# Moving the load of the next queries behind the round trip of denominators on SyncE's queue

## The reference, cut to what matters

```python
x = x + layernorm(attn(layernorm(x)))
x = x + layernorm(ffn(layernorm(x)))
# attn, for each of 16 heads of 32 numbers:
q_phi = exp(features(q) - |q|^2 / 2)            # 128 features
S, sum_k = k_phi^T v, sum over rows of k_phi    # per sequence
out = (q_phi S) / max(q_phi sum_k, eps)         # a denominator for each row and head
attn = concat(out) w_out^T
# ffn: sigmoid gates, top 4 of 32 experts, capacity 512, plus a shared expert
```

## Time and profile before

| | |
|---|---|
| median of 3 runs | 2131.26 us (2128.41 to 2144.04) |
| the profiled execution, its time | 2139.98 us |
| the profiled execution, its span | 2138.2 us |
| mean granted TensorE clock in it | 0.939 of full speed |
| fused stage, about | 862 to 1417 us of the span |

### The profile page before, as it was taken

How to read it: one execution, slowest core, us unless ns; L and a number is a source line. 1 busy time by engine, 2 the same in 40 slices (tenths; PEclk the granted TensorE clock), 3 DMA queues, 4 the chain that set the end, 5 groups by cost and what they waited for, 6 DMA issues and landing times.

```text
span 2138.2 us, 33516 instructions
## 1 busy us (share of the span) xinstructions
PE 1843.4 (86%) x12976; PEld 892.7 (42%) x12976; DVE 1183.8 (55%) x2055; ACT 1071.0 (50%) x1371; POOL 756.9 (35%) x716
## 2 busy tenths in 40 slices
PE   8899999999988999699789888635998999987785
PEld 6444444444436888133233333322444444443231
DVE  7676766666650000156778878762444444445786
ACT  5555554545524666566566666412444444432443
POOL 0000000000000000013578787875677777761110
PEclk9999999999998999899899999867999999998897
DMA  6636354454527888567887785443799999987983
GB/s 231 232 124 239 132 193 178 168 203 165 178 103 209 211 212 205 120 175 188 225 221 239 220 235 183 161 183 100 169 197 221 247 241 246 205 146 241 334 288 126
DMA packets 197295, 421.92 MB, mean 197 GB/s; under 512 B 34068, under 2 KB 72340, under 8 KB 180512
## 3 DMA queue, kind: packets, MB, share of 16 engines
q1 hardware_dynamic: 91632, 239.19, 38.1%
q10 hardware_dynamic: 68640, 124.26, 16.5%
q0 software_dynamic: 36864, 56.32, 14.2%
HBM read 237.06 MB, written 193.86 MB: 202 GB/s over the span
## 4 chain that ended last, share of the span: by engine, by line
DMA 16%; PE 11%; DVE 10%; issue 9%; POOL 7%; ACT 3%; SPq 1%; POOLq 0%; DVEq 0%; ACTq 0%
DMA acc_dram<-s_y,s_slot 6%; DMA s_spread<-share_dram 5%; POOL acc_dram L1427 3%; PE s_gates L1486 2%; PE s_y L922 2%; PE s_ups L1486 2%; POOL slot_dram L1261 2%; DMA share_dram<-s_share 2%; DVE s_heads L1121 2%; PE s_ys L1501 1%; DMA s_dens<-den_dram 1%; DMA den_dram<-s_den 1%; DVE s_stats L1652 1%; DVE s_x L1675 1%; PE s_logits L891 1%
## 5 line engine op out<-in xcount | busy, mean ns | idle before, releaser
L271 PE MATMUL s_proj<-s_xT,keep_wqkv 128*128 128x512 f16 x1536 | 343.5, 380 | 0.0
L1261 POOL DMA_INDIRECT slot_dram<-keep_filled,keep_slots x256 | 274.1, 1071 | 76.2 <-issue 73.5
L1427 POOL DMA_INDIRECT acc_dram<-s_y,s_slot x128 | 204.5, 1597 | 92.7 <-issue 36.2
L271 PEld LDWEIGHTS s_proj<-s_xT,keep_wqkv 128*128 128x128 f16 x1536 | 148.2, 98 | 184.5 <-issue 14.8
L922 PE MATMUL s_y<-keep_wo,s_at_hl 128*128 128x512 f16 x768 | 197.2, 412 | 19.2 <-DVE s_x L1133 19.0
L250 PE MATMUL s_proj<-keep_wqkv,s_xT 128*128 128x512 f16 x768 | 181.4, 395 | 32.4 <-ACT s_xT L524 32.4
L1541 ACT ACTIVATE s_gate<-s_gates 128x512 f32<-128x512 f32 x96 | 57.1, 597 | 264.6 <-PE s_ups L1486 223.6
L1611 DVE SCALAR_TENSOR_TENSOR s_h<-s_gate,s_ups 128x512 f32<-128x512 f32 x96 | 65.9, 686 | 215.0 <-ACT s_gate L1541 215.0
L542 ACT ACTIVATE s_hl<-s_rot 128x1024 f16<-128x1024 f32 x64 | 67.6, 1057 | 231.3 <-DVE s_rot L413 230.5
L991 ACT ACTIVATE s_phi<-s_logits 128x1024 f32<-128x1024 f32 x128 | 131.5, 1027 | 99.2 <-PE s_logits L891 98.4
L400 DVE TENSOR_TENSOR s_by_cos<-s_proj,s_table 128x1024 f32<-128x1024 f32 x64 | 78.3, 1224 | 185.5 <-PE s_proj L271 184.4
(11 more groups left out here) (166 smaller groups left out, 3154.9 us busy)
## 6 DMA issues: line engine op xcount, KB each, us to landing
qk_dram<-s_hl ACTq DMA_DIRECT2D x32, 1024.0 KB
keep_ahead<-qk_dram SPq DMA_DIRECT2D x48, 512.0 KB
acc_dram<-s_zero SPq DMA_DIRECT2D x17, 1024.0 KB, 13.1
v_dram<-s_v ACTq DMA_DIRECT2D x16, 1056.0 KB
s_v<-v_dram SPq DMA_DIRECT2D x16, 1056.0 KB
s_x<-x_in SPq DMA_DIRECT2D x16, 1024.0 KB
xc_dram<-s_x SPq DMA_DIRECT2D x16, 1024.0 KB
s_spread<-share_dram SPq DMA_DIRECT2D x64, 256.0 KB
```

What stands on the lines that cost most here:

```text
L271: mm = nc.tensor.matmul(out[:, 512 * b:512 * b + 512], left, right, start=(c == 0 and i == 0), stop=(c == EC - 1 and i == 2))
L1261: nc.gpsimd.indirect_dma_start(out=io["slot"], out_offset=bass.IndirectOffsetOnAxis(ap=slots[n % 2][:, a * K + j:a * K + j + 1], axis=0), ...
L1427: nc.gpsimd.indirect_dma_start(out=io["acc"], out_offset=bass.IndirectOffsetOnAxis(ap=slot[e % RING][:, a, 0:1], axis=0), in_=y[e % 2][:, ...
```

## The change

In iteration n, the load of the queries of group n + 1 is issued after the round trip of group n - 1, not ahead of it. The load of the first odd group ahead of the loop and the load of the residual rows behind the round trip stay where they are. Nothing else is changed: the same transfers, of the same sizes, with the same waits.

```diff
             load_q(1)
             for n in range(1, NG + 1):
+                spread_share(n - 1)
                 if n + 1 < NG:
                     load_q(n + 1)
-                spread_share(n - 1)
                 load_x(n - 1)
```

## The result

The changed kernel takes 2200.39 us (median of 4 runs, 2198.91 to 2209.46) against 2132.96 us before (4 runs, 2128.41 to 2144.04): ratio 1.0311, 95% interval 1.028 to 1.0341, 67 us slower. The profiled execution has a span of 2197.1 us, 58.9 more than before, at a mean granted clock of 0.928. All of it lies in the fused stage: the division of group 15 starts at 1414.70, and it started at 1355.35. The forecast was 2176, with 2155 to 2199 as its own range: the direction came out, and the time lies 1.4 us above the upper end of that range.

What follows compares the result with a forecast made beforehand. The prediction took a closed ring of waits in the fused stage, 30.4 us a group, as the bound. Ten groups at 4.0 - 0.3 us (37) plus 8 for groups 2 to 5 gave 45 us: 2176 us, range 2155 to 2199.

Steps and rivals of the forecast that it cites:

- What bounds the kernel, and what moves: Fused stage: a closed ring of waits bounds it, 30.4 us a group; the change asks for queries one whole group later.
- ring of three legs: Fused-stage lap from one group's division to the next, 30.4 us; lengthening one part without shortening another is paid each group.
- The first leg: From the division of group 5 to the second logits of group 7: 5.2 us before, forecast 9.2, plus 4.0 a group.
- When they arrive: Queries' load behind the spread: 1.61 MB at 0.217 MB a us, arriving 7.0 us after the division may start, bounds 6.0 to 8.7.
- First logits to second: TensorE after the queries arrive: 2.2 us, the middle of 1.7 (clock kept) and 2.8 (clock at its lower level).
- What it gives back: Denominators' small stores, freed of the queries' load, get faster; gain taken as 0.3 us a group, bounds 0 and 2.0.
- the second leg: From a group's second logits to the reciprocals: 12.9 us before, forecast 0.3 us shorter a group.
- The third leg: From the reciprocals to the next division, the share store and 1 MB of spread: 11.7 us, forecast unchanged.
- The sum: Whole kernel: 37 us for ten groups plus 8 us for groups 2 to 5, 45 us in all, giving 2176 us.
- Faster by the small stores: Rival: queries at most 4 us after the spread, round trip 2 us shorter each time, 28 us gained: 2103 us; 5%.
- No change: Rival: queries near 6 us late, cost regained at the reciprocals, or orders hardly differ: 2131 to 2150 us; 14%.
- The third rival: ScalarE's store of rows shares the engines with the queries, up to 2.6 us later in 14 groups: 2212 us; 8%.

## Why the prediction was right, and where its sizes were off

**What bounds the kernel, and what moves.** Right. The ring of three legs is what both profiles show, and the load of queries is asked for one group later than its place in the text suggests. The run with a third buffer shows it: with the old deadline in the new place the time is that of before. The sizes fell short: the profile grew by 58.9 us and the median by 67, where 45 were forecast, and 2200.39 lies just above the forecast's range of 2155 to 2199. The first leg is 11.25 us and was to be 9.2; TensorE's waits for queries are 102.7 us and were to be some 70.

**When they arrive.** The step that failed in size, by the largest amount. The term was 7.0 us with 6.0 to 8.7 as bounds; it measured 8.42, and 7.33 to 9.15 in the single laps. The rate was right (0.214 MB a us in the window of 1209 to 1216, and 0.24 between the two sizes of load). Missing was a part that does not go with bytes, 0.9 us by the first rate and 1.7 by the second. The prediction divided the bytes by the mean rate of 16 engines, but a waiter waits for the last of them. The windows of before show that the lone load of group 1 was still under way in its ninth microsecond:

```profile
868.00:873.00 5.00, 3.68 (x12) 0.50 1.08 229
873.00:874.00 1.00, 1.00 (x6) 0.50 0.76 156
874.00:875.00 1.00, 1.00 (x5) 0.50 0.31 66
```

(length, TensorE busy and count, clock, DMA share, GB/s), full share until 873 and then a tail of 2 us. The packets of the changed kernel show the tail behind the spread too, since the queries move in packets of 8 KB and the residual rows behind them in packets of 2 KB. From 1215 to 1216 and from 1217 to 1218:

```profile
DMA packets 48, 0.23 MB, mean 227 GB/s; under 512 B 12, under 2 KB 12, under 8 KB 23
DMA packets 114, 0.23 MB, mean 231 GB/s; under 512 B 4, under 2 KB 4, under 8 KB 113
```

The first packet of residual rows starts at 1215.66, and one last packet of the queries still runs until 1217.74. In the mean of the eight laps the residual rows start 5.2 us after the division, the last packet of queries ends at 7.2, and the first logits follow at 8.4. So some of the engines are through 2.0 us before the last one. (The 1.2 us from the last packet to the logits has a like in the spread, whose last packet starts 1.4 to 1.8 us ahead of the division in before.) How much of the missing part is this tail no run separates; that it is not the small last transfer is shown.

**First logits to second.** 2.2 us predicted, 2.83 measured: the upper bound. The first logits took 1.03 us, the low level of 1.2 GHz, in all eight laps, after 6.1 to 8.4 us of idle time. I had about 4 us of idle time and took the middle between both levels. My own arrival says more than 4: 1059.9 in place of 1054.40 is 5.5 us. And at 4 us the rows of before would not have decided: the logits behind 3.64 us took 1.03, those behind 3.59 us took 0.61. The laps of the run with extra matmuls that kept the clock put its price at about 2 us in the first two legs.

**What it gives back.** 0.3 us a group predicted in the second leg, 1.0 measured, and not for the reason given. The small stores do take 2.5 us and not 4.5 in the changed kernel, but the time from the denominators to the reciprocals did not shrink (9.45 before, 9.68 after), because VectorE's list sets it. The leg is shorter since the denominators are read 2.56 us behind the second logits and no more 3.80: VectorE, which had its low half to finish first, now waits for TensorE. And the stores are faster since they are issued at 1224.64, after ScalarE's store of rows is through (at 1223.5), where in before that store runs beside them. The queries are hardly beside them in either: in before their last packets end at 1063.6, 1 us behind the issue of the small stores.

**The third leg** was left at zero change: 11.91 and 11.70.

**The sum.** Per lap 30.35 + (8.42 - 7.0) + (2.83 - 2.2) - (1.0 - 0.3) + 3.7 - 0.2 = 35.2, which is what the laps have: + 4.8 in place of + 3.7. The larger gain of the second leg hid a part of what the first was short of, and that is luck. Ten laps, from the division of group 4 to that of group 14, took 48.9 us more; 37 were predicted. The opening took 10.9 more (1032.89 for 1021.97) where I had 8. The profiled executions differ by 59, the medians by 67; the kernel's own difference is known to the interval only, 60 to 73 us.

**The rivals.** Faster by the small stores: the changed kernel has them 2 us faster, and the reciprocals follow the denominators no sooner (9.68 and 9.45 us); the third buffer has the place and no gain. No change: the arrival was near 6 us in no lap, 7.33 at the least. The third rival took the Trainium skill's rule (DMA: Bandwidth & Descriptors, Queues, rings and completion order: turns between queues, packet by packet). Its mechanism did not decide: ScalarE's store of rows was issued at 1212.37 and had its first packet at 1218.26, and until the queries were through only q1 moved anything of size, as before. From 1209 to 1216 in the changed kernel:

```profile
q1 hardware_dynamic: 235, 1.50, 100.4%
```

Behind the queries, though, from 1219 to 1223, with the residual rows in q1 and the store in q10, both move in the same microseconds:

```profile
q10 hardware_dynamic: 451, 0.90, 65.7%
q1 hardware_dynamic: 232, 0.44, 29.7%
```

So the trace has both, turns between queues and order of issue. Here the rule agrees, there it doesn't, and what makes the difference was not tried. For this change the order of issue was the right guide to the direction.

## What to carry to other kernels

Read where a load is issued in time, not in the text: a queue that waits makes "ahead of the round trip" mean "after the last one", and moving the call behind the next round trip moves it by a whole period. A prefetch that is off the critical path costs nothing where it stands, and pays nothing when it is moved away, until its slack is gone; then it costs its bytes, the tail of the slowest DMA engine, and the clock that TensorE loses while it waits (here some 2 us in the first two legs of a lap). In a ring whose transfers follow each other closely, a transfer taken out of one leg is easily given back in the next one, so cost all legs.

## What was not expected of the hardware

- Of a load of 1.61 MB behind a spread some engines were through 2.0 us before the last one (mean of eight laps), and its waiter waits for the last.
- 32 KB took 7.5 us when a load of queries stood ahead in the same queue and ScalarE's stores ran beside, and 1.5 us else (a share store issued at 1231.48 was followed by the next issue at 1232.95 in the run with the load ahead of the spread).
- 24 extra matmuls, 5.3 us of work, in each wait of TensorE kept the clock in four of eight laps; in two it was low at the first logits, in two it fell behind them.
- Two queues were seen to share the DMA engines within the same microseconds, and in the same lap one of them moved nothing for the 6 us after its issue.
- A lap shorter by 0.8 us in one profile (numerators three times, store a step earlier) went with no shorter time: 2132.95 us.
